# Two-stage transformer kernel on one core: the layers' steps in other orders, multi-query statistics one by one behind the maxima, the first queries' turned copy on VectorE

## The chip, the core and the metric

One core of one Trainium2 chip runs the kernel. The metric is the device time of one execution in microseconds (us). Engines are called by their names: TensorE (PE in the profile; PEld is its weight load), VectorE (DVE), ScalarE (ACT), GpSimd (POOL) and SyncE (SP), which issues transfers.

## What is computed

The input x is 8 sequences of 512 tokens with 128 features. Two blocks follow, each added to x behind a layer norm:

```python
x = x + _layernorm(_L0_attn_ref(_layernorm(x), ...))     # multi-query attention, 16 heads of 8, one k and v
x = x + _layernorm(_L0_ffn_ref(_layernorm(x), ...))      # six layers
# one of the six layers
x = attn_layer(shift_tokens(x), Wqkv[i], q_scale[i], k_scale[i], Wo[i]) + x
x = ffn_layer(shift_tokens(x), ln_g[i], ln_b[i], W1[i], b1[i], W2[i], b2[i]) + x
# attn_layer: 16 heads of 64; q and k are normalised to length 1, scaled, rotated;
# attention is causal within windows of 32 tokens and the window before
# ffn_layer: layer norm, x @ W1 in halves a and gate, a * gelu(gate) @ W2
```

All is float32. Where it can, the kernel splits an operand into a rounded part and a remainder (hi and lo) and multiplies in three passes.

## The kernel before

**Stages.** A constants stage, the multi-query stage (to about 650 us), the layers (about 670 to 3740 us) and an output stage. Each engine runs a program of its own, in the order in which it is written; engines meet by semaphores alone. `Events` counts them: `at(k, cycle)` is the value of a semaphore once k of its events of that cycle are done.

**Multi-query stage.** It goes through 8 batches of 512 tokens, in a loop whose body is `sequence`. Of each of 16 heads (`g` is a group of four, `i` a head in it) TensorE computes the scores in two layouts. `scores` writes four tiles (`qt`), alternately into the banks `score[0]` and `score[1]`; VectorE's `maxima` takes the row maxima, five heads (AHEAD) before `scoresT`, the other layout, uses them and ScalarE's `exps` takes exponentials. A score tile waits for the maximum of the tile two before it (`s_max`). Between heads VectorE does the three norms: 0 of the next batch's input, 1 of the batch before's projected output, 2 of its residual sum. Each is `mean_and_var` (four bn_stats, four bn_aggr, an addition), then a power on GpSimd (`inverse_deviation`, L272), then `normalised` (four tensor_scalar), one lump each behind the maxima of a head. At the end of a batch the next one's keys and queries are turned: `turn_keys` and `turn_queries` on TensorE into bank `turn[0]`; the keys are copied out half by ScalarE (`keys_turned`), half by VectorE (`other_keys`, L660), each of the four groups of queries by ScalarE (`queries_turned`, the first one behind the exponentials of head (3, 3)). TensorE's first score of the next batch waits for the first queries' copy.

**Layers.** A step (cycle) takes 256 tokens, that is two tiles of 128; 6 layers x 16 steps = 96 cycles. `CYCLE` writes out by hand, for each engine, the order of its tokens in a cycle. The number behind a token is the tile against the cycle's own, so that a negative one belongs to an earlier cycle's tile; tile 2 of one cycle is tile 0 of the next. On TensorE: Pq, Pk, Pv project (six matmuls each, L1228 to L1230) into the one PSUM tile `proj`; Tq, Tk turn rotated q and k (L1237); S scores (L1256), X turns the exponentials (L1263), V weights the values (L1277), O turns the result (L1284), W projects it (L1291); mean (L1301), var (L1307), spread (L1314), GG, AA (L1323 to L1325) and F4 (L1332) are the feed-forward layer. All but the projections, S and spread write a ring of two PSUM buffers in turn, so each waits until the one before the last is released (`RELEASE`). On ScalarE: XSa loads the projection's input, Qq and Qk square `proj` (L1384), EV copies the values out of it, EQ, EK, EX, EO copy ring buffers out, MK writes the mask, IG makes the guess for the inverse root (L1395), EXP the exponentials, GEL gelu with two table loads. On VectorE: Cq, Ck rotate (L1494, L1496), and wait for the square; Rq, Rk sum squares, MX takes maxima, SB subtracts them, RS sums and inverts, R weights, AM gates (L1591), WX and XN add to x (XN: L1597), XC, FV, XM belong to the norm. On GpSimd: Aq, Ak add (L1142), Mq, Mk scale (L1148), N is Newton's steps, XSd, XL remainders, FP a power. A projection waits until `proj` is rotated or copied. SyncE moves the values into `v_win` (VM). `NEXT_WEIGHTS` puts pieces of the next layer's weights (hi_, lo_ halves, turn_ tables) ahead of certain tokens, two and one cycles before a layer ends.

## Time and profile before

| | us |
|---|---|
| median of 3 timed runs | 3786.93 (3782.76 to 3786.98) |
| the profiled execution | 3777.28 |
| its span, first to last instruction | 3775.5 |

| engine | busy us | share of the span |
|---|---|---|
| PE | 3506.6 | 93% |
| PEld | 2890.2 | 77% |
| DVE | 2982.0 | 79% |
| ACT | 2678.1 | 71% |
| POOL | 2407.2 | 64% |

Busy time is that of the instructions' spans; matmuls are pipelined, so neighbours overlap and a busy TensorE is not TensorE at its peak. A shape's start-to-start step says what it costs. A value like "[0.17 <-DVE by_sin L1496]" behind a row is the idle time ahead of it and what ended that. The granted clock is given as a share of TensorE's full clock.

### The profile page before, as it was taken

Reading aid. Unit: us, or ns where it says so; the run is one execution under the profiler, and the core shown is the slowest. Engines: PE = TensorE matmul, PEld = TensorE weight load, DVE = VectorE, ACT = ScalarE, POOL = GpSimd, SP = SyncE. Lnnn points to the kernel's source line nnn. Section 1 sums busy time; section 2 is a strip of 40 time slices with the busy share of each in tenths; the row PEclk is TensorE's granted clock in tenths of the full one; section 3 lists DMA queues with packets and bytes.
Section 4 is the critical chain, followed back from the end, with each engine's and each line's share of the span. In section 5 each row is a group of like instructions: output and inputs, shape, how many; then the busy total and the mean of one; then the engine's idle time right before and its main releaser. Section 6 shows DMA issues by size and latency. Waiting matters only on the chain. (4 is left out here: it accounts for less than half of the span.)

```text
span 3775.5 us, 161676 instructions
## 1 busy us (share of the span) xinstructions
PE 3506.6 (93%) x67234; PEld 2890.2 (77%) x67234; DVE 2982.0 (79%) x4293; ACT 2678.1 (71%) x4155; POOL 2407.2 (64%) x2884
## 2 busy tenths in 40 slices
PE   5988898599999999999999999999999999999995
PEld 3555555378888888888888888888888888888884
DVE  4455554588888888888888888888888888888884
ACT  2444443377778788887878888888888888878872
POOL 1010000577777777787777777777877777777773
PEclk9999999799999999999999999999999999999997
DMA  1000000132222232222322223222232222222222
GB/s 55 4 3 3 5 3 6 40 91 68 67 68 66 73 93 69 70 65 74 90 67 67 67 72 90 67 67 67 72 90 67 67 69 65 74 67 70 69 66 63
DMA packets 161717, 227.93 MB, mean 60 GB/s; under 512 B 42258, under 2 KB 60632, under 8 KB 161496
## 3 DMA queue, kind: packets, MB, share of 16 engines
q1 hardware_dynamic: 161624, 226.85, 24.0%
q8 instruction: 38, 0.62, 0.1%
q14 instruction: 55, 0.45, 0.0%
HBM read 21.00 MB, written 4.19 MB: 7 GB/s over the span
## 5 line engine op out<-in xcount | busy, mean ns | idle before, releaser
L1142 POOL TENSOR_TENSOR by_cos<-by_cos,by_sin 128x1024 f32<-128x1024 f32 x384 | 916.4, 2386 | 38.5 <-DVE by_sin L1496 38.5
L1148 POOL TENSOR_TENSOR by_cos<-by_cos,norms 128x1024 f32<-128x1024 f32 x384 | 724.8, 1910 | 0.0
L1494 DVE TENSOR_TENSOR by_cos<-proj,turns 128x1024 f32<-128x1024 f32 x384 | 470.0, 1224 | 224.0 <-ACT squares L1384 223.4
L1228 PE MATMUL proj<-qkv_hi,xs_hib 128*128 128x512 f32 x1152 | 522.4, 453 | 52.5 <-DVE by_sin L1496 39.8
L1384 ACT ACTIVATE squares<-proj 128x1024 f32<-128x1024 f32 x384 | 392.4, 1022 | 174.1 <-PE proj L1230 168.3
L1364 ACT ACTIVATE vb<-proj 128x1024 f32<-128x1024 f32 x192 | 195.3, 1017 | 422.9 <-PE proj L1230 383.0
L1496 DVE TENSOR_TENSOR by_sin<-proj,turns 128x1024 f32<-128x1024 f32 x384 | 466.1, 1214 | 0.0
L1500 DVE TENSOR_REDUCE sumsb<-squares 128x16 f32<-128x1024 f32 x384 | 463.9, 1208 | 1.5 <-DVE w_lo L1563 1.5
L1229 PE MATMUL proj<-qkv_lo,xs_hib 128*128 128x512 f32 x1152 | 457.3, 397 | 1.3 <-issue 1.3
L1230 PE MATMUL proj<-qkv_hi,xs_lob 128*128 128x512 f32 x1152 | 458.0, 398 | 0.0
L1237 PE MATMUL ring<-ident,by_cos 128*128 128x128 f32 x3072 | 403.7, 275 | 1.7 <-POOL by_cos L1148 1.4
L1237 PEld LDWEIGHTS ring<-ident,by_cos 128*128 128x128 f32 x3072 | 351.2, 142 | 49.0 <-DVE attnb L1531 22.4
L668 DVE TENSOR_REDUCE a_row_max<-a_score 128x1 f32<-128x128 f32 (+3 forms) x512 | 238.1, 487 | 175.2 <-PE a_score L311 171.2
L1291 PE MATMUL ring<-attnT,wo 128*128 128x256 f32 x1536 | 347.6, 379 | 1.4 <-ACT attnT L1364 1.2
L1228 PEld LDWEIGHTS proj<-qkv_hi,xs_hib 128*128 128x128 f32 x1152 | 218.6, 190 | 141.0 <-DVE by_sin L1496 93.0
L1291 PEld LDWEIGHTS ring<-attnT,wo 128*128 128x128 f32 x1536 | 284.3, 190 | 36.6 <-issue 1.4
L1256 PE MATMUL score<-kTb,qTb 64*32 64x64 f32 x24576 | 286.2, 226 | 8.4 <-issue 8.4
L1277 PE MATMUL ring<-v_win,pTb 64*32 64x64 f32 x24576 | 285.6, 225 | 6.5 <-issue 6.5
L509 ACT ACTIVATE a_probs<-a_scoreT 128x512 f32<-128x512 f32 (+1 forms) x384 | 186.3, 532 | 142.5 <-PE a_scoreT L324 137.0
L1256 PEld LDWEIGHTS score<-kTb,qTb 64*32 64x32 f32 x24576 | 256.8, 105 | 27.4 <-issue 10.6
L272 POOL TENSOR_TENSOR a_rstdb<-a_varb,minus_half 128x4 f32<-128x4 f32 x24 | 24.2, 1008 | 397.4 <-DVE a_varb L622 397.4
L1277 PEld LDWEIGHTS ring<-v_win,pTb 64*32 64x32 f32 x24576 | 254.3, 105 | 25.5 <-issue 23.9
(174 smaller groups left out, 8217.5 us busy)
## 6 DMA issues: line engine op xcount, KB each, us to landing
v_win<-vb SPq DMA_DIRECT2D x1152, 128.0 KB, 2.4
v_win<-vb SPq DMA_DIRECT2D x768, 64.0 KB, 2.0
in_qkv<-L_ffn_Wqkv SPq DMA_DIRECT2D x12, 768.0 KB
wo<-L_ffn_Wo SPq DMA_DIRECT2D x6, 512.0 KB, 4.1
x_tok<-L_attn_x SPq DMA_DIRECT2D x8, 256.0 KB, 4.8
residual<-x_tok SPq DMA_DIRECT2D x8, 256.0 KB, 2.1
o_x<-residual SPq DMA_DIRECT2D x1, 2048.0 KB, 7.8
out<-o_x SPq DMA_DIRECT2D x8, 256.0 KB, 2.3
```

The lines of the kernel that those rows point to most:

```text
L1142: nc.gpsimd.tensor_tensor(both, both, by_sin[:, j, :], ALU.add).then_inc(e[f"{w_}_added"].sem, 1)
L1148: nc.gpsimd.tensor_tensor(heads, heads, inverse, ALU.mult).then_inc(e[f"{w_}_ready"].sem, 1)
L1228: nc.tensor.matmul(out, xs_hi[:, tile], qkv_hi[:, cols], start=True, stop=False)
L1229: nc.tensor.matmul(out, xs_hi[:, tile], qkv_lo[:, cols], start=False, stop=False)
L1230: last = nc.tensor.matmul(out, xs_lo[:, tile], qkv_hi[:, cols], start=False, stop=True)
L1237: last = nc.tensor.transpose(out[:, i * P:(i + 1) * P], by_cos[:, t % 2, j, i * P:(i + 1) * P], ident[:, :])
L1256: last = nc.tensor.matmul(score[queries, at:at + KEYS], qT[rows, t % 2, i, queries], keys, start=False, stop=True, skip_group_check=True)
L1277: last = nc.tensor.matmul(out[queries, at:at + DH], pT[rows, i, queries], v_win[rows, t % 2, n, i, :], start=True, stop=True)
L1291: last = nc.tensor.matmul(out[:, 0:HS], wo[:, i, :], attnT[:, i, :], start=(i == 0), stop=(i == PAIRS - 1))
L1494: nc.vector.tensor_tensor(of_heads(by_cos[:, t % 2, j, :]), heads, table(0), ALU.mult)
L1496: nc.vector.tensor_tensor(swapped, heads, table(1), ALU.mult).then_inc(e[f"{w_}_rotated"].sem, 1)
L1500: nc.vector.tensor_reduce(sums[:, t % 2, j, :, 0], squares[:, :].rearrange("p (h d) -> p h d", d=DH), AX.X, ALU.add).then_inc(e[f"{w_}_sum ...
```

## The change

It has three parts.

1. `CYCLE` gets other orders on the four computing engines, and `NEXT_WEIGHTS` other places. On TensorE, V:-2 goes to the front and Tq:0 from the front to behind Pq:2; mean goes behind X:-1; S:0 ahead of O:-2, V:-1 and var; W:-1 ahead of Tk:1. On ScalarE, EX:0 of the end becomes EX:-2 at the front; XSa:3 goes from the front to behind Qk:2; EQ:0, XF, FSQ and XH move. On VectorE, XC goes behind Rq:2, WX ahead of Rq:3, and MX:1 and SB:1 ahead of Rk:3 and XN. On GpSimd, Aq of the second tile goes to the front of the next cycle (Aq:1), Mq:0 behind XSd:2, Mk:1 behind XL. No work is added or removed.
2. In the multi-query stage a bn_stats stands behind each of the four maxima of a head, and the normalising instructions behind the second (tile 0), third (tile 1) and fourth (tiles 2 and 3) maximum of another head. What is left of the lump is `variance`. Since a norm's tiles stand in the maxima of the head at the same place, `normalised` now waits for the inverse deviation behind the second maximum instead of the fourth.
3. The copy of the first group of turned queries goes from ScalarE (`queries_turned(b, 0)`) to VectorE (`first_queries`), with an event of its own (`q_first`).

```diff
-        "t1_full": Events(sem("a_t1_full"), 5), "t1": Events(sem("a_t1"), 5), "k_half": Events(sem("a_k_half"), 1),
+        "t1_full": Events(sem("a_t1_full"), 5), "t1": Events(sem("a_t1"), 4), "q_first": Events(sem("a_q_first"), 1), "k_half": Events(sem("a_k_half"), 1),
...
-                turned(b, 0, stacked(g), "t1_full", ("t1", g + 2, 1))
+                turned(b, 0, stacked(g), "t1_full", ("t1", g + 1, 1) if g else ("q_first", 1, 1))
...
-                pe.wait_ge(e["t1"].sem, e["t1"].at(2, b + 1))
+                pe.wait_ge(e["q_first"].sem, e["q_first"].at(1, b + 1))
...
-                        elif (g, i) == (3, 3):
-                            queries_turned(b, 0)
...
+            def statistics(b, norm, tiles, after, t):
+
+                if t == 0:
+                    dve.wait_ge(padded, 2)
+                    if after:
+                        dve.wait_ge(e[after].sem, e[after].at(1, b))
+                last = nc.vector.bn_stats(stat6[:, norm, t, :], tiles[t])
+                if t == TILES - 1:
+                    last.then_inc(e[f"stats{norm}"].sem, 1)
...
+            def normal_tile(b, norm, out, tiles, t):
+
+                if t == 0:
+                    dve.wait_ge(e[f"rstd{norm}"].sem, e[f"rstd{norm}"].at(1, b))
+                return nc.vector.tensor_scalar(out[:, t, :], tiles[t], stat[:, norm, t, 0:1], rstd[:, norm, t:t + 1],
+                                               ALU.subtract, ALU.mult)
...
+            def first_queries(b):
+
+                dve.wait_ge(e["t1_full"].sem, e["t1_full"].at(2, b + 1))
+                nc.vector.tensor_copy(qT0[:, 0, :], turn[0][:, :]).then_inc(e["q_first"].sem, 1)
...
-            def maxima(b, g, i):
+            def maxima(b, g, i, behind=None):
...
+                    if behind:
+                        behind(qt)
...
+            def norm_behind(b, norm, out, tiles, done):
+
+                def behind(qt):
+                    for t in {1: (0,), 2: (1,), 3: (2, 3)}.get(qt, ()):
+                        last = normal_tile(b, norm, out, tiles, t)
+                        if t == TILES - 1:
+                            last.then_inc(e[done].sem, 1)
+                return behind
...
+                        behind = None
+                        if not first:
+                            if (g, i) == (0, 0):
+                                behind = lambda qt: statistics(b - 1, 1, projected, "proj", qt)
+                            elif (g, i) == (0, 1):
+                                behind = norm_behind(b - 1, 1, o, projected, "o")
+                            elif (g, i) == (0, 3):
+                                behind = lambda qt: statistics(b - 1, 2, tiles_of(b - 1), "x2", qt)
+                            elif (g, i) == (1, 0):
+                                behind = norm_behind(b - 1, 2, y, tiles_of(b - 1), "y")
+                        if not last:
+                            if (g, i) == (1, 3):
+                                behind = lambda qt: statistics(b + 1, 0, tiles_of(b + 1), None, qt)
+                            elif (g, i) == (2, 0):
+                                behind = norm_behind(b + 1, 0, xn, tiles_of(b + 1), "xn")
...
-    "PE": "Tq:0 V:-2 Pq:2 mean Tk:0 X:-1 O:-2 Pk:2 var V:-1 S:0 spread Pv:2 O:-1 Tq:1 Pq:3 Tk:1 W:-1 Pk:3 GG "
+    "PE": "V:-2 Pq:2 Tq:0 Tk:0 X:-1 mean Pk:2 S:0 O:-2 V:-1 var Pv:2 spread O:-1 Tq:1 Pq:3 W:-1 Tk:1 Pk:3 GG "
     "S:1 AA X:0 Pv:3 F4",
-    "Act": "XSa:2 XSa:3 EV:1 EQ:0 IG:1 XF EXP:-1 Qq:2 FSQ EK:0 EX:-1 MK:0 EO:-2 Qk:2 EV:2 EO:-1 EQ:1 Qq:3 IG:2 "
-    "MK:1 XH EXP:0 EK:1 Qk:3 GEL EX:0",
-    "DVE": "R:-2 XC Cq:2 Rq:2 RS:-1 FV Ck:2 R:-1 XM Rk:2 MX:0 SB:0 Cq:3 Rq:3 RS:0 WX:-1 Ck:3 AM Rk:3 XN MX:1 "
-    "SB:1",
-    "Pool": "Mq:0 XSd:2 N:1 Ak:1 Aq:2 FP Mq:1 Mk:1 XSd:3 Ak:2 XL N:2 Aq:3 Mk:2",
+    "Act": "EX:-2 XSa:2 EV:1 XF IG:1 EXP:-1 Qq:2 EQ:0 EK:0 MK:0 EX:-1 FSQ Qk:2 XSa:3 EO:-2 EV:2 EO:-1 XH EQ:1 "
+    "IG:2 Qq:3 EXP:0 MK:1 EK:1 Qk:3 GEL",
+    "DVE": "R:-2 Cq:2 Rq:2 XC RS:-1 Ck:2 FV R:-1 XM Rk:2 MX:0 SB:0 Cq:3 WX:-1 Rq:3 RS:0 Ck:3 AM MX:1 SB:1 Rk:3 "
+    "XN",
+    "Pool": "Aq:1 XSd:2 Mq:0 N:1 Ak:1 Aq:2 Mq:1 XSd:3 FP Ak:2 XL Mk:1 N:2 Mk:2",
...
-    "Act": {(-2, "Qq:3"): "hi_q1", (-2, "EK:1"): "hi_q0", (-2, "GEL"): "hi_k0", (-2, "EX:0"): "hi_k1",
-          (-1, "XSa:3"): "hi_v0", (-1, "EXP:-1"): "hi_v1"},
-    "DVE": {(-2, "WX:-1"): "lo_q0", (-2, "Rk:3"): "turn_3", (-2, "XN"): "lo_k1", (-2, "SB:1"): "lo_k0",
-          (-1, "Cq:2"): "turn_0 turn_1 turn_2"},
-    "Pool": {(-2, "XL"): "lo_q1", (-1, "N:1"): "lo_v0", (-1, "Aq:2"): "lo_v1"},
+    "Act": {(-2, "EXP:0"): "hi_q0", (-2, "EK:1"): "hi_q1", (-2, "GEL"): "hi_k0", (-1, "XSa:2"): "hi_v0",
+          (-1, "EV:1"): "hi_k1", (-1, "XF"): "hi_v1"},
+    "DVE": {(-2, "AM"): "lo_q0 turn_0 turn_1", (-2, "Rk:3"): "turn_2 turn_3", (-1, "R:-2"): "lo_k1",
+          (-1, "RS:-1"): "lo_v1"},
+    "Pool": {(-2, "Mk:2"): "lo_q1", (-1, "Aq:1"): "lo_k0", (-1, "XSd:2"): "lo_v0"},
```

## Rows read from the trace of the kernel before

**Rows 1.** Two stretches: length, busy us (xcount) of PE, PEld, DVE, ACT, POOL, clock, DMA, GB/s.
```profile
40.00:648.00 608.00, 541.43 (x3799) 347.76 (x3797) 333.00 (x999) 271.15 (x596) 57.31 (x29) 0.97 0.01 3
...
1000.00:3600.00 2600.00, 2542.12 (x55110) 2187.03 (x55109) 2272.08 (x2718) 2085.62 (x3078) 2011.80 (x2438) 1.00 0.29 72
```

**Rows 2.** Timeline of PE in one cycle of the layers: start us, us, what.
```profile
2020.51 1.04 PE L1237 MATMUL ring<-ident,by_cos 128*128 128x128 f32 x8
...
2021.48 1.48 PE L1277 MATMUL ring<-v_win,pTb 64*32 64x64 f32 x128
...
2022.89 0.50 PE L1228 MATMUL proj<-qkv_hi,xs_hib 128*128 128x512 f32 x1
...
2028.21 0.50 PE L1228 MATMUL proj<-qkv_hi,xs_hib 128*128 128x512 f32 x1
...
2030.14 1.48 PE L1277 MATMUL ring<-v_win,pTb 64*32 64x64 f32 x128
...
2031.53 1.47 PE L1256 MATMUL score<-kTb,qTb 64*32 64x64 f32 x128
...
2032.93 0.43 PE L1314 MATMUL ring<-ident,f_rstdb 128*128 128x128 f32 x2
...
2033.53 0.50 PE L1228 MATMUL proj<-qkv_hi,xs_hib 128*128 128x512 f32 x1 [0.17 <-DVE by_sin L1496]
...
2035.02 1.06 PE L1284 MATMUL ring<-ident,attnb 128*128 128x128 f32 x8
...
2035.92 1.04 PE L1237 MATMUL ring<-ident,by_cos 128*128 128x128 f32 x8
...
2036.71 0.48 PE L1228 MATMUL proj<-qkv_hi,xs_hib 128*128 128x512 f32 x1
...
2042.34 0.58 PE L1228 MATMUL proj<-qkv_hi,xs_hib 128*128 128x512 f32 x1
...
2048.61 0.48 PE L1228 MATMUL proj<-qkv_hi,xs_hib 128*128 128x512 f32 x1
...
2051.38 1.04 PE L1237 MATMUL ring<-ident,by_cos 128*128 128x128 f32 x8
```

**Rows 3.** Timeline of ACT and DVE behind the projection at 2022.89.
```profile
2024.76 1.01 ACT L1384 ACTIVATE squares<-proj 128x1024 f32<-128x1024 f32 x1
...
2025.80 1.22 DVE L1494 TENSOR_TENSOR by_cos<-proj,turns 128x1024 f32<-128x1024 f32 x1 [0.36 <-ACT squares L1384]
2026.94 1.22 DVE L1496 TENSOR_TENSOR by_sin<-proj,turns 128x1024 f32<-128x1024 f32 x1
```

**Rows 4.** Groups of instructions by line, whole span: busy us, mean ns, idle before.
```profile
L1591 DVE SCALAR_TENSOR_TENSOR hidden<-ring,ffn_col,hidden 128x256 f32<-128x256 f32 (+1 forms) x288 | 121.4, 477 | 30.8 <-PE ring L1325 30.2
...
L1395 ACT ACTIVATE norms<-floors,guess_bias 128x32 f32<-128x32 int32 x192 | 60.6, 316 | 0.0
...
L1597 DVE TENSOR_TENSOR xT<-ring,xT 128x256 f32 (+1 forms) x96 | 40.7, 424 | 94.2 <-PE ring L1332 94.2
...
L272 POOL TENSOR_TENSOR a_rstdb<-a_varb,minus_half 128x4 f32<-128x4 f32 x24 | 24.2, 1008 | 397.4 <-DVE a_varb L622 397.4
...
L660 DVE CAST a_kT<-a_turn 32x512 fp32r<-32x512 f32 x16 | 11.1, 693 | 7.1 <-PE a_turn L376 7.0
```

**Rows 5.** Timeline of PE at a boundary between two multi-query batches.
```profile
268.00 0.65 PE L376 MATMUL a_turn<-ident,a_qa 128*128 128x128 f32 x4 [0.18 <-DVE a_kT L660]
270.15 0.32 PE L310 MATMUL a_score<-a_kT,a_qT 128*128 128x128 f32 x1 [1.50 <-ACT a_qT L501]
```

**Rows 6.** Waits of PE, 286 to 325 us: us in total, times, longest.
```profile
PE a_score L310 <- DVE a_row_max L668: 3.5, 5, 0.9
```

**Rows 7.** Two stretches of the multi-query stage, columns as in rows 1.
```profile
290.00:303.00 13.00, 10.79 (x70) 7.50 (x68) 11.73 (x44) 7.01 (x15) 1.06 (x2) 1.00 0.05 20
...
344.00:348.00 4.00, 3.65 (x18) 1.81 (x22) 1.27 (x3) 0.22 (x1) 2.80 (x1) 0.52 0.00 0
```

**Rows 8.** A cycle in which the next layer's weights are prepared, columns as in rows 1.
```profile
1175.00:1207.00 32.00, 30.17 (x625) 25.38 (x627) 29.24 (x38) 25.82 (x41) 26.82 (x32) 1.00 0.27 66
```

More of the change, by code:

```diff
@@ L433, in sequence @@
                 pe.wait_ge(e["k1"].sem, e["k1"].at(1, b))
-                pe.wait_ge(e["t1"].sem, e["t1"].at(5, b))
+                pe.wait_ge(e["t1"].sem, e["t1"].at(4, b))
                 for g in range(GROUPS):
@@ L488, in _ @@
                 turn_queries(-1, g)
-            pe.wait_ge(e["t1"].sem, e["t1"].at(3, 0))
+            pe.wait_ge(e["t1"].sem, e["t1"].at(2, 0))
             for i in range(PER_GROUP):
@@ L596, in _ @@
             keys_turned(-1)
-            for g in range(GROUPS):
+            for g in range(1, GROUPS):
                 queries_turned(-1, g)
@@ L605, in _, with variance @@
             dve.wait_ge(padded, 2)
-            def mean_and_var(b, norm, tiles, after=None):
-                stats = e[f"stats{norm}"]
-                dve.wait_ge(padded, 2)
-                if after:
-                    dve.wait_ge(e[after].sem, e[after].at(1, b))
-                for t, tile in enumerate(tiles):
-                    last = nc.vector.bn_stats(stat6[:, norm, t, :], tile)
-                last.then_inc(stats.sem, 1)
+            def statistics(b, norm, tiles, after, t):
[6 more added lines that the diff above has]
+                    last.then_inc(e[f"stats{norm}"].sem, 1)
+            def variance(b, norm):
+                stats = e[f"stats{norm}"]
                 dve.wait_ge(stats.sem, stats.at(1, b))
@@ L623, in mean_and_var @@
                                         ALU.add).then_inc(e[f"var{norm}"].sem, 1)
+            def mean_and_var(b, norm, tiles, after=None):
+                for t in range(TILES):
+                    statistics(b, norm, tiles, after, t)
+                variance(b, norm)
+            def normal_tile(b, norm, out, tiles, t):
[3 more added lines that the diff above has]
+                                               ALU.subtract, ALU.mult)
             def normalised(b, norm, out, tiles):
-                dve.wait_ge(e[f"rstd{norm}"].sem, e[f"rstd{norm}"].at(1, b))
-                for t, tile in enumerate(tiles):
-                    last = nc.vector.tensor_scalar(out[:, t, :], tile, stat[:, norm, t, 0:1], rstd[:, norm, t:t + 1],
-                                                   ALU.subtract, ALU.mult)
+                for t in range(TILES):
+                    last = normal_tile(b, norm, out, tiles, t)
                 return last
@@ L692, in add_output @@
                 nc.vector.tensor_tensor(four, four, o[:, :, :], ALU.add).then_inc(e["x2"].sem, 1)
+            def norm_behind(b, norm, out, tiles, done):
+                def behind(qt):
+                    for t in {1: (0,), 2: (1,), 3: (2, 3)}.get(qt, ()):
+                        last = normal_tile(b, norm, out, tiles, t)
+                        if t == TILES - 1:
+                            last.then_inc(e[done].sem, 1)
+                return behind
             def sequence(b, first=False, last=False):
@@ L697, in sequence @@
                         then = g * PER_GROUP + i + AHEAD
+                        behind = None
[13 more added lines that the diff above has]
+                                behind = norm_behind(b + 1, 0, xn, tiles_of(b + 1), "xn")
                         if then < MQA_H:
-                            maxima(b, then // PER_GROUP, then % PER_GROUP)
+                            maxima(b, then // PER_GROUP, then % PER_GROUP, behind)
                         if i == 2 and g + 1 < GROUPS:
@@ L706, in sequence @@
                             if (g, i) == (0, 0):
-                                mean_and_var(b - 1, 1, projected, "proj")
-                            elif (g, i) == (0, 1):
-                                normalised(b - 1, 1, o, projected).then_inc(e["o"].sem, 1)
+                                variance(b - 1, 1)
                             elif (g, i) == (0, 2):
@@ L712, in sequence @@
                             elif (g, i) == (0, 3):
-                                mean_and_var(b - 1, 2, tiles_of(b - 1), "x2")
-                            elif (g, i) == (1, 0):
-                                normalised(b - 1, 2, y, tiles_of(b - 1)).then_inc(e["y"].sem, 1)
+                                variance(b - 1, 2)
                         if last:
@@ L718, in sequence @@
                         if (g, i) == (1, 3):
-                            mean_and_var(b + 1, 0, tiles_of(b + 1))
-                        elif (g, i) == (2, 0):
-                            normalised(b + 1, 0, xn, tiles_of(b + 1)).then_inc(e["xn"].sem, 1)
+                            variance(b + 1, 0)
                         elif g == 3 and i < 2:
@@ L725, in sequence @@
                             other_keys(b)
+                        elif (g, i) == (3, 3):
+                            first_queries(b)
                 if last:
@@ L748, in _ @@
             other_keys(-1)
+            first_queries(-1)
             for i in range(PER_GROUP):
```

## The prediction

> **What bounds the kernel now.** I read the page's slices first: TensorE is the fullest engine everywhere but in the fill around 650 to 780 us. Then two stretches by windows [rows 1]: in the layers TensorE is busy 2542 of 2600 us at a granted clock of 1.00, VectorE 87%, ScalarE 80%, GpSimd 77%; in the multi-query stage (40 to 648 us) TensorE is busy 541 of 608 us at a mean clock of 0.97. So time can only come from TensorE's gaps, and from work that a low clock stretches. The chain of waits on the page covers only the output stage and doesn't help; the timeline of one cycle does [rows 2]. The 96 cycles of the layers repeat with one period: transposes of Tq:0 start at 2020.51 and again at 2051.38, 30.87 us. An uninterrupted projection with what follows it starts its successor at a fixed step, so I take start-to-start steps rather than durations (matmuls overlap by some 0.1 us).
>
> **The loop through `proj`.** One PSUM tile `proj` serves all six projections of a cycle. Behind Pq (2022.89) ScalarE squares it (2024.76, 1.01 us), VectorE rotates it twice (2025.80 and 2026.94, 1.22 us each, end 2028.16) and only then Pk may start: 2028.21 [rows 2, 3]. That is 5.32 us from a projection that is rotated to the next, whatever TensorE does meanwhile. Between Pq:2 and Pk:2 the old order has mean, Tk, X and O to fill it; their issue steps are too short, so it waits some 0.7 us. Between Pk:2 (2028.21) and Pv:2 (2033.53) it has var, V, S and spread; again 5.32, with a wait on the rotation in the row of 2033.53. Elsewhere the work between two projections is longer than the rotation.
>
> **Layers: the new order, stretch by stretch** (steps from rows 2; numbers behind tokens are tiles).
> - Pq:2 to Pk:2. Old and new hold about 3.0 us of work (new: Tq:0, Tk:0, X:-1, mean), less than the 3.8 that the rotation leaves. Stays 5.32.
> - Pk:2 to Pv:2. New: S:0, O:-2, V:-1, var. Pk with var 2028.21 to 2030.14 = 1.93; S 2031.53 to 2032.93 = 1.40; O 2035.02 to 2035.92 = 0.90; V 2021.48 to 2022.89 = 1.41. Sum 5.64, over 5.32: TensorE is no longer late for the rotation, and 0.32 longer than before.
> - Pv:2 to Pq:3. Old O:-1 and Tq:1, 2033.53 to 2036.71 = 3.18. New has spread too, two of the transposes of which Tq takes 0.11 each (0.89/8): 3.40. ScalarE's copy of `proj` is done long before.
> - Pq:3 to Pk:3 (W and Tk:1 change places) and Pk:3 to Pv:3 (unchanged): 2036.71 to 2048.61 = 11.90, the latter with GEL's wait.
> - Pv:3 to the next Pq:2. Old F4, Tq:0, V:-2: 2048.61 to 2051.38 and 2020.51 to 2022.89 = 5.15. Tq:0 (2020.51 to 2021.48 = 0.97) has moved behind Pq:2, into the wait: 4.18.
>
> Sum 5.32 + 5.64 + 3.40 + 11.90 + 4.18 = 30.44, against 30.87: 0.43 us a cycle. The gain is not O or V as such: what stood in an over-full stretch (Tq:0 between Pv:3 and Pq:2) goes where TensorE waited. I then followed each queue through the new cycle with Pq:2 at 0. Ring buffers: X:-1 needs EQ:0, which starts behind Qq:2 and ends at 3.7, so X starts then and not at 3.25, but ends before Pk:2 at 5.32. Mean needs EK:0 (4.7). EO:-2 frees var's buffer at 10.3, var starts at 10.4. XM frees Tq:1's buffer at 13.2, Tq:1 starts at 13.4. EX:-2 now opens ScalarE's cycle and has V:-2 waiting a microsecond after it. GpSimd's new order keeps Mq:0 0.8 us and Mk:1 1 us ahead of their transposes. SyncE's transfers into v_win are issued, as now, most of a cycle before their V. Everything hides, but with 0.1 to 0.3 us in five places; I take the sum and keep 0.1 to 0.7 us a cycle for the range. With some 91 full cycles: 39 us (9 to 64).
>
> **Layer boundary.** The same 16 weight pieces (ScalarE 6, GpSimd 3, VectorE 3 and 4 tables) go to other places. A preparing cycle now has TensorE busy 30.17 of 32 us [rows 8], so such a cycle loses about 1.1 us to the regular one, and I count about three in each of five boundaries. VectorE gets lo_q0 and two tables ahead of AM, where F4 waits for them, but loses the run of three ahead of the first Cq:2. I take nothing, plus or minus 8 us in all.
>
> **Multi-query stage, first queries.** At each of seven batch boundaries TensorE has the first queries turned by 268.65 and waits until 270.15: the copy is queued on ScalarE behind three exponentials [rows 5]. VectorE is idle there. Its nearest copy out of PSUM (32 partitions, 512 columns) is 0.69 us [rows 4], so the copy is there at 268.65 + 0.1 + 0.69 = 269.5 and 0.65 us goes: 7 x 0.65 = 4.6. Behind it on VectorE stand only the maxima, which need that copy anyway.
>
> **Statistics one by one.** In the 39 us around a batch's norms TensorE waits 3.5 us in five waits for maxima behind a lump of VectorE work [rows 6]. Four of them lie where VectorE is itself nearly full (11.73 of 13 us [rows 7]): spreading out the same instructions frees at most the 1.3 us of its gaps. And the new order makes a wait: the first normalised tile stands behind the second maximum, while the inverse deviation takes GpSimd 1.0 us [rows 4] from the variance on; VectorE would stand about 0.5 us, with two maxima and so TensorE's next score behind it, at norms 1 and 2. I take no gain there (-0.6 to +1.0), and 0.7 us at norm 0, where TensorE's heads are longer than VectorE's load: 7 x 0.7 = 5. The Trainium skill, Perfetto Trace Analysis, Optimizing Scalar/DVE Operations, says that breaking up instructions may let work complete sooner if Vector isn't saturated but causes bubbles. By it nearly all 3.5 us would go, 25 us in seven batches; the row of the 13 us speaks against its condition. That is a rival below.
>
> **Clock.** The trace grants 0.52 (a mix of the levels 2.4 and 1.2 GHz) in 344 to 348 us [rows 7], just behind a boundary wait of the kind of rows 5; such a drop stands behind six of the seven. Its 3.65 us of work would take some 1.9 less at 2.4 GHz. With 0.85 instead of 1.5 us idle some drops should go: I take half, 6 x 1.9 / 2 = 5 (0 to 11).
>
> **Sum.** Layers 39, first queries 5, statistics 5, clock 5: 54 us. The profiled execution took 3777.3 (span 3775.5), 9.6 less than the median 3786.9 of the three timed runs. 3777.3 - 54 = 3723; against the median 3733.
>
> **Rivals.**
> - The fill is paid elsewhere: a second loop becomes the bound. Rk:3 and its floors now stand behind SB:1, and the guess IG:1, EXP:-1 and Qq:2 wait for them. From Pk:3: rotation done 5.27; AM 3 x 0.477 = 1.43 [rows 4]; MX, SB, Rk at 1.22 each; floors and guess 0.32 each; EXP and square at 1.01 each; Cq 2.36: 15.4 and some 0.3 of handoffs to Pk:2. From there TensorE needs 5.64 + 3.40 and Pq:3 to Pk:3, 5.63: 30.4, as much as TensorE's own sum. At 0.4 more the layers gain nothing and only the 15 us of the first stage are left: 3772.
> - The same loop on the other side, slower: if it closes at over 31.04 us (30.87 and 15/91), the kernel is slower than before. It has about 20 handoffs between three engines; 0.05 more at each and the misfit of one VectorE operation make 31.3: 0.43 x 91 = +39, less 15: 3811. For it speaks that slack is nearly nothing; against it, that the old order had VectorE wait for F4 1 us in each cycle (94 us in 96 [rows 4]) with MX:1 and SB:1 behind it, and that XN now stands last.
> - The skill's rule holds, all maxima waits go: 20 us more, 3713.
> - The change doesn't do what it says: TensorE's wait at the boundary isn't for the copy but for what comes next on ScalarE (exponentials, then V). Costs the 10 us of queries and clock, 3743; inside the forecast.
>
> **How the numbers follow.** Forecast 3733 with 0.66 (its terms alone: 3705 to 3765); layers gain nothing 0.12; slower 0.11; rule 0.11. Range 3702 to 3775, leaving out 0.11 above, some of the 3772 case, and little below. 0.2% is 7.6 us, about what a measurement can tell from no change. Faster: 0.66, 0.11 and half of 0.12, say 0.82; same 0.07; slower 0.11.
>
> **What would show it.** Period between two Tq:0 at 30.3 to 30.6; no wait on by_sin ahead of Pv:2; Pq:2 to Pk:2 still 5.3. If EXP:-1 ends later than Pq:2, the second loop binds. At the batch boundary the wait ends 0.6 earlier, by VectorE; mean clock of 40 to 648 over 0.97; VectorE standing for a_rstdb before a_ob and a_yb. The forecast is wrong if the period stays at 30.9, or if boundary cycles grow past 33.

## The result and the profile after

| us | median | lowest to highest | runs |
|---|---|---|---|
| before | 3782.06 | 3777.72 to 3786.98 | 6 |
| after | 3756.27 | 3744.30 to 3766.11 | 6 |

The ratio is 0.9927, with a 95% interval of 0.9916 to 0.9939: faster by 26 us, less than half of the 54 that were forecast, and inside the range. The profiled execution of after has a span of 3742.5 us where that of before had 3775.5, 33 less; it is the fastest of its six. In after the lines of the layers stand 42 further down (L1228 is L1270, L1237 is L1279), the maxima are L687 and the maximum's neighbours L611 (bn_stats), L637 (normalising), L671 (the first queries' copy) and L678 (the keys' copy).

The two stretches of [rows 1] in after:

```profile
40.00:648.00 608.00, 542.52 (x3819) 349.40 (x3818) 344.96 (x1038) 271.57 (x594) 66.68 (x40) 0.96 0.01 5
...
1000.00:3600.00 2600.00, 2533.26 (x55104) 2177.23 (x55103) 2302.20 (x2717) 2111.84 (x3080) 2003.81 (x2442) 1.00 0.29 72
```

In the second row TensorE is idle 67 of 2600 us (2600 - 2533.26), where it was 58: there are new waits in the layers. In the first row a fixed window misleads: the stage is shorter now and 40 to 648 us holds the start of the fill (the pipeline of the layers starting up) with its low clock; to 626 us the clock is 0.98.

**Where the 33 us are.** I cut both traces at the first and the last matmul of mean (L1301 before, L1343 after): 779.02 and 3729.63 in before, 750.64 and 3696.86 in after. So 28.4 us went ahead of the layers and only 4.4 of their 2950.6 us. The forecast had it the other way round: 15 and 39. One pair of profiles is thin for the second number: with the old orders three profiles (before, e2_queries, e3_stats) have 2950.6 to 2960.7 us there, with the new ones four (after, e0_again, e1_layers, e7_later) 2946.2 to 2950.2, so the layers gave 4 us by this pair and some 10 by the middle of either group. The steps from one mean matmul to the next split the 4.4 again. The regular cycle (its median) fell from 30.93 to 30.68 (medians of 95 steps), worth 95 x 0.25 = 24 us; but at each of the five layer boundaries the eight cycles around it now take 7.4 us more than regular ones, where it was 3.3 (at the last one 9.7 and 5.3): 5 x 4.1 = 20 us back.

**The cycle.** TensorE's timeline of the cycle of [rows 2] in after (start us, us, what):

```profile
2020.30 1.48 PE L1319 MATMUL ring<-v_win,pTb 64*32 64x64 f32 x128
2021.71 0.50 PE L1270 MATMUL proj<-qkv_hi,xs_hib 128*128 128x512 f32 x1
...
2023.21 1.91 PE L1279 MATMUL ring<-ident,by_cos 128*128 128x128 f32 x16
2025.54 1.09 PE L1305 MATMUL ring<-ident,probs 128*128 128x128 f32 x8 [0.42 <-ACT qTb L1406]
2026.46 0.69 PE L1343 MATMUL ring<-xfb,mean_of 128*128 128x256 f32 x2
2026.94 0.50 PE L1270 MATMUL proj<-qkv_hi,xs_hib 128*128 128x512 f32 x1
...
2028.53 1.48 PE L1298 MATMUL score<-kTb,qTb 64*32 64x64 f32 x128
2029.95 1.09 PE L1326 MATMUL ring<-ident,attnb 128*128 128x128 f32 x8
2030.97 1.48 PE L1319 MATMUL ring<-v_win,pTb 64*32 64x64 f32 x128
2032.39 0.61 PE L1349 MATMUL ring<-mean_of,fsqb 128*128 128x1 f32 x4
2032.85 0.48 PE L1270 MATMUL proj<-qkv_hi,xs_hib 128*128 128x512 f32 x1
...
2036.22 0.48 PE L1270 MATMUL proj<-qkv_hi,xs_hib 128*128 128x512 f32 x1
...
2048.11 0.48 PE L1270 MATMUL proj<-qkv_hi,xs_hib 128*128 128x512 f32 x1
```

The wait on the rotation ahead of Pv:2 (2032.85) is gone, and X's 0.42 on EQ stands where the forecast put it. EXP:-1 ends at 2023.28 on ScalarE and Qq:2 starts at 2023.47, when the projection is done. Start to start: Pq:2 to Pk:2 5.23 (forecast 5.32), Pk:2 to Pv:2 5.91 (5.64), Pv:2 to Pq:3 3.37 (3.40), Pq:3 to Pv:3 11.89 (11.90), and to the next Pq:2 4.28 (4.18). One stretch carries the miss. In it P takes 1.59 to the next start, S 1.42, O 1.02, V 1.42, var 0.46. In the old order the forecast had read P with var as 1.93 (now 2.05) and O as 0.90.

**The layer boundary.** TensorE's waits in 1122 to 1157 us, across a cycle that prepares the next layer's weights:

```profile
PE ring L1374 <- DVE hidden L1633: 1.3, 1, 1.3
PE ring L1279 <- DVE xT L1639: 1.0, 1, 1.0
PE ring L1279 <- DVE attnb L1573: 0.6, 1, 0.6
PE ring L1305 <- ACT hidden L1506: 0.5, 1, 0.5
```

Three of the four, 2.9 us, are for VectorE, and the longest is that of F4 for AM, which now has lo_q0 and two tables ahead of it. What VectorE and GpSimd do there:

```profile
1142.15 2.37 POOL L1184 TENSOR_TENSOR by_cos<-by_cos,by_sin 128x1024 f32<-128x1024 f32 x1
...
1142.56 2.51 DVE L1585 TENSOR_TENSOR qkv_lo<-in_qkv,qkv_hi 128x512 fp32r<-128x512 f32 x1
...
1144.99 0.75 DVE L1593 SCALAR_TENSOR_TENSOR turns<-tables_sb,in_qs 128x256 f32<-128x256 f32 x2
...
1145.66 0.47 DVE L1633 SCALAR_TENSOR_TENSOR hidden<-ring,ffn_col,hidden 128x256 f32<-128x256 f32 x1
```

And the same instruction over the whole span, first in after, then in before (duration in ns: shortest, median, longest):

```profile
L1585 DVE TENSOR_TENSOR qkv_lo<-in_qkv,qkv_hi x18: 679/2492/2509, 646.3 to 3151.3; 128x512 fp32r<-128x512 f32 x18
```

```profile
L1543 DVE TENSOR_TENSOR qkv_lo<-in_qkv,qkv_hi x18: 628/720/1748, 673.7 to 3173.5; 128x512 fp32r<-128x512 f32 x18
```

An instruction of 0.7 us takes 2.5 where it meets GpSimd's addition of 2.4 us, and ends 0.55 us behind it (1145.07 against 1144.52). Two of the three in a boundary do: lo_q0, and lo_v1 16 us later, behind which TensorE waits 1.45 us for the rotation ahead of Pv. The Trainium skill, SBUF — State Buffer, section SBUF: two separate sides, says that VectorE and GpSimd share a pair of ports under an exclusive lock: a VectorE instruction with two SBUF inputs and a GpSimd instruction that reads SBUF don't run together, and whichever comes second waits for the whole of the other. The trace agrees: 0.68 becomes 2.51 only where such a GpSimd instruction is running. This rule spoke against the new places, and the prediction had not weighed it.

**The multi-query stage.** A batch boundary of after (260.76 answers [rows 5]), and the first norm behind it:

```profile
259.25 0.65 PE L376 MATMUL a_turn<-ident,a_qa 128*128 128x128 f32 x4 [0.18 <-DVE a_kT L678]
...
259.94 0.69 DVE L671 CAST a_qT<-a_turn 128x512 fp32r<-128x512 f32 x1 [0.82 <-PE a_turn L376]
...
260.76 0.32 PE L310 MATMUL a_score<-a_kT,a_qT 128*128 128x128 f32 x1 [0.86 <-DVE a_qT L671]
```

```profile
285.94 0.62 DVE L687 TENSOR_REDUCE a_row_max<-a_score 128x1 f32<-128x128 f32 x2
287.14 0.41 DVE L637 TENSOR_SCALAR a_ob<-a_turn,a_stat,a_rstdb 128x128 f32<-128x128 f32 x1 [0.57 <-POOL a_rstdb L272]
```

The boundary wait ends by VectorE and lasts 0.86 instead of 1.50. VectorE stands 0.57 for the inverse deviation, as forecast. TensorE's waits for maxima over 40 to 640 us, in before, then in after:

```profile
PE a_score L310 <- DVE a_row_max L668: 34.2, 66, 0.9
```

```profile
PE a_score L310 <- DVE a_row_max L687: 18.5, 58, 0.6
```

15.7 us of such waiting are gone, where the forecast had 5. The 39 us of [rows 6], at the same place in a batch of after (423 to 462 us), show where:

```profile
PE a_score L310 <- DVE a_row_max L687: 1.3, 4, 0.5
```

That is 2.2 us less in each batch: 0.6 at norm 0, as forecast (0.79 to 0.22), and 1.5 at norms 1 and 2 (2.68 to 1.22), where the forecast had taken no gain. GpSimd's addition to the turned keys marks each batch once. Of the six batches between the second mark and the eighth, only one of before went by without a low clock, 268.10 to 342.29, 74.2 us; in after three did, 71.6 us each:

```profile
333.75 4.54 POOL L281 TENSOR_TENSOR a_kT<-a_kT,ones 128x2048 fp32r<-128x2048 f32 x1 [23.22 <-DVE a_kT L678]
...
405.38 4.54 POOL L281 TENSOR_TENSOR a_kT<-a_kT,ones 128x2048 fp32r<-128x2048 f32 x1 [23.23 <-DVE a_kT L678]
...
477.07 4.53 POOL L281 TENSOR_TENSOR a_kT<-a_kT,ones 128x2048 fp32r<-128x2048 f32 x1 [23.23 <-DVE a_kT L678]
```

(The batch from 333.75 to 405.38 and the next; the third ends at 548.71.) That is 2.6 us a batch without any help of the clock. The six batches together take 458.6 us in before and 436.7 in after, 21.9 less: 6 x 2.6 = 15.6 by the shorter waits, and 6.3 because fewer and shorter stretches of low clock fall into them.

### The profile page after: what moved, and what is told of

Read it like the earlier page. It is cut to its first block and busy times, and to the rows that moved or that the text cites. A ratio compares the mean times of both kernels' runs of the same rounds, so it can differ in the third digit from the quotient of the medians.

```text
span 3742.5 us, 161624 instructions
## 1 busy us (share of the span) xinstructions
PE 3489.5 (93%) x67234; PEld 2872.1 (77%) x67234; DVE 3020.8 (81%) x4301; ACT 2705.2 (72%) x4147; POOL 2398.5 (64%) x2884
## 5 line engine op out<-in xcount | busy, mean ns | idle before, releaser
L1190 POOL TENSOR_TENSOR by_cos<-by_cos,norms 128x1024 f32<-128x1024 f32 x384 | 733.5, 1910 | 13.0
L1270 PE MATMUL proj<-qkv_hi,xs_hib 128*128 128x512 f32 x1152 | 512.4, 445 | 49.2 <-DVE by_sin L1538 40.2
L1279 PE MATMUL ring<-ident,by_cos 128*128 128x128 f32 x3072 | 385.3, 273 | 8.4 <-DVE xT L1639 5.5
L1279 PEld LDWEIGHTS ring<-ident,by_cos 128*128 128x128 f32 x3072 | 351.0, 142 | 34.3 <-issue 7.6
L687 DVE TENSOR_REDUCE a_row_max<-a_score 128x1 f32<-128x128 f32 (+3 forms) x512 | 240.3, 486 | 127.9 <-PE a_score L311 121.6
L1333 PEld LDWEIGHTS ring<-attnT,wo 128*128 128x128 f32 x1536 | 292.3, 190 | 44.0 <-ACT attnT L1406 1.4
L1198 POOL TENSOR_TENSOR xs_lob<-xsb,xs_hib 128x128 fp32r<-128x128 f32 x192 | 88.3, 460 | 347.7 <-ACT xs_hib L1406 347.7
L1270 PEld LDWEIGHTS proj<-qkv_hi,xs_hib 128*128 128x128 f32 x1152 | 219.1, 190 | 109.9 <-DVE by_sin L1538 63.3
```

The source lines that it names most:

```text
L1190: nc.gpsimd.tensor_tensor(heads, heads, inverse, ALU.mult).then_inc(e[f"{w_}_ready"].sem, 1)
L1270: nc.tensor.matmul(out, xs_hi[:, tile], qkv_hi[:, cols], start=True, stop=False)
L1279: last = nc.tensor.transpose(out[:, i * P:(i + 1) * P], by_cos[:, t % 2, j, i * P:(i + 1) * P], ident[:, :])
L1333: last = nc.tensor.matmul(out[:, 0:HS], wo[:, i, :], attnT[:, i, :], start=(i == 0), stop=(i == PAIRS - 1))
```

## The experiments

The theory drawn from these profiles had four parts: the new order of the layers gives 0.25 us a cycle and not 0.43, since steps ahead of the small matmuls are longer; the weight pieces cost 4 us a boundary, of which the shared port is a part; the statistics give more than their term; and the clock makes the rest. The rivals are named with each run. Each run was timed against the kernel before on the same chip.

| kernel | median us | ratio to before, 95% interval | regular cycle | boundary, over regular |
|---|---|---|---|---|
| after, again (e0_again) | 3750.71 | 0.9909 [0.9896, 0.9923] | 30.68 | 7.4 |
| e1_layers | 3775.56 | 0.9985 [0.9975, 0.9994] | 30.68 | 7.4 |
| e2_queries | 3779.14 | 0.9993 [0.998, 1.0005] | 30.93 | 3.3 |
| e3_stats | 3773.82 | 0.9979 [0.997, 0.9987] | 30.95 | 3.2 |
| e4_ports | 3748.40 | 0.9911 [0.9891, 0.9931] | 30.68 | 5.8 |
| e5_together | 3743.43 | 0.9900 [0.9885, 0.9914] | 30.50 | 9.2 and 7.6 |
| e6_weights | 3738.39 | 0.9879 [0.9865, 0.9894] | 30.68 | 4.2 |
| e7_later | 3758.50 | 0.9924 [0.9906, 0.9942] | 30.68 | 7.4 |
| e9_both | 3731.09 | 0.9868 [0.9851, 0.9885] | 30.50 | 4.3 |
| e10_gelu | 3740.16 | 0.9895 [0.9875, 0.9916] | 30.50 | 8.1 to 9.2 |

The last two columns come from the steps between mean matmuls in each profile. The last is for the first four boundaries; the fifth varies more (7.5 to 12.8 us with the new orders). They agree to 0.1 us between profiles of the same order, save where a low clock falls into a preparing cycle: one boundary of e7_later (9.0 us), two of the first four of e5_together and all of e10_gelu. The first stage moves more: the layers of the kernels that share after's first stage begin anywhere from 746 to 762 us, by the number of batches with a low clock. So an edit in the layers is read from its cycles first and from the median second.

**e1_layers: part 1 alone** (the new `CYCLE` and `NEXT_WEIGHTS` in the kernel before).

```diff
-    "PE": "Tq:0 V:-2 Pq:2 mean Tk:0 X:-1 O:-2 Pk:2 var V:-1 S:0 spread Pv:2 O:-1 Tq:1 Pq:3 Tk:1 W:-1 Pk:3 GG "
+    "PE": "V:-2 Pq:2 Tq:0 Tk:0 X:-1 mean Pk:2 S:0 O:-2 V:-1 var Pv:2 spread O:-1 Tq:1 Pq:3 W:-1 Tk:1 Pk:3 GG "
...
+    "DVE": {(-2, "AM"): "lo_q0 turn_0 turn_1", (-2, "Rk:3"): "turn_2 turn_3", (-1, "R:-2"): "lo_k1",
+          (-1, "RS:-1"): "lo_v1"},
```

> The kernel before with the layers' new orders and weight places alone. From the two traces: the regular cycle goes from 30.90 to 30.68 us (75 regular cycles, 17 us less) and the three irregular cycles at each of five layer boundaries from 3.4 to 7.4 us in excess (20 us more); the fill gains some 5. Theory (the layers bring next to nothing, the gain is the first stage's): 0 to 9 us less than before. Rival (the orders bring the gain and the first stage's smaller time is chance of the clock): over 20 us less.

Measured: 7 us less than before (3782.49 in 29 runs), cycle 30.68, 7.4 us over at each boundary; from the first to the last mean matmul 2947.2 against 2950.6. The largest term of the sum, 39 us, is worth 3 us by the profile and 7 by the medians, and it is the layers by themselves that lose it, not something that the other two parts do to them.

**e2_queries: part 3 alone.**

```diff
-                        elif (g, i) == (3, 3):
-                            queries_turned(b, 0)
...
+                        elif (g, i) == (3, 3):
+                            first_queries(b)
```

> The kernel before with the first queries' copy on VectorE alone. The boundary wait goes from 1.50 to 0.86 us seven times, 4.5 us. Theory: on top of that the clock drops behind that wait go from six to two or fewer, some 2 us each: 8 to 14 us less than before. Rival (the drops have nothing to do with that wait): 4 to 5 us less, and still five or six drops behind the boundaries.

Measured: 3.3 us less, with an interval that includes no change. The seven waits fell from 10.5 us in sum to 6.0:

```profile
PE a_score L310 <- DVE a_qT L656: 6.0, 7, 0.9
```

A batch without a low clock takes 73.5 us (from GpSimd's addition at 490.30 to that at 563.84) against 74.2: 0.7 a batch, the size in the sum. None of its low stretches stands right behind a boundary wait any more, but four stand later in the batch, so the clock gave nothing on top. The size is the rival's, 4 to 5 us, and not the theory's 8 to 14.

**e3_stats: part 2 alone.**

```diff
-                                mean_and_var(b - 1, 1, projected, "proj")
-                            elif (g, i) == (0, 1):
-                                normalised(b - 1, 1, o, projected).then_inc(e["o"].sem, 1)
...
+                            if (g, i) == (0, 0):
+                                behind = lambda qt: statistics(b - 1, 1, projected, "proj", qt)
+                            elif (g, i) == (0, 1):
+                                behind = norm_behind(b - 1, 1, o, projected, "o")
```

> The kernel before with the statistics and the normalising instructions behind single maxima alone. TensorE's waits for maxima at score L310 fell from 34.2 to 18.5 us between the two traces of the first stage. Theory: this part alone brings those 16 us, less what VectorE stands for the inverse deviation (0.57 us a time, in 14 places): 8 to 16 us less. The prediction's term (no gain at norms 1 and 2, 0.7 at norm 0): 5 us less. Drops of the clock behind the boundary wait stay at five to seven.

Measured: 8.7 us less. The waits for maxima fall to 19.4 us, VectorE stands for the inverse deviation 4.0 us at each of the three norms:

```profile
PE a_score L310 <- DVE a_row_max L684: 19.4, 60, 0.6
```

```profile
DVE a_ob L639 <- POOL a_rstdb L272: 4.0, 7, 0.6
```

In its profile six batches take 75.0 or 75.1 us, each with two low stretches. Columns as in [rows 7]; the first stretch is behind the boundary wait of 1.50, the second 17 us later:

```profile
345.00:349.00 4.00, 3.86 (x22) 1.21 (x21) 1.23 (x3) 0.00 (x0) 2.28 (x1) 0.60 0.00 0
...
361.00:365.00 4.00, 4.00 (x21) 3.12 (x19) 0.72 (x2) 0.33 (x1) 0.00 (x0) 0.73 0.00 0
```

The profiled execution was 9 us longer than this kernel's median, so its clock is not typical; the waits are. A batch of before with two low stretches of the same length at nearly the same places (419.18 to 496.19 us) takes 77.0 us. Like against like, then, part 2 alone gives 1.9 us a batch. The three parts alone give 6.9 + 3.3 + 8.7 = 19 us; together they gave 26 and, once more on another chip, 33 (e0_again). The intervals of the four ratios together leave some 8 us open either way, so the surplus of 7 is no finding and that of 14 is one. It goes the way of the clock, since the profiles of after and e0_again have three and five of the six batches free of a low clock where before has one; that nothing else makes it isn't shown.

**e4_ports: after, with the two residuals moved away from GpSimd's additions.**

```diff
-    "DVE": {(-2, "AM"): "lo_q0 turn_0 turn_1", (-2, "Rk:3"): "turn_2 turn_3", (-1, "R:-2"): "lo_k1",
-          (-1, "RS:-1"): "lo_v1"},
+    "DVE": {(-2, "WX:-1"): "lo_q0", (-2, "AM"): "turn_0 turn_1", (-2, "Rk:3"): "turn_2 turn_3", (-1, "R:-2"): "lo_k1",
+          (-1, "Cq:2"): "lo_v1"},
```

> The changed kernel with two of VectorE's three subtractions of the next weights (lo_q0, lo_v1) moved from where GpSimd is in an addition of two SBUF tensors (2.4 us long) to where GpSimd does Newton's short steps: lo_q0 ahead of WX:-1, lo_v1 ahead of Cq:2. Same number of instructions. Theory (a VectorE instruction with two SBUF inputs stands until GpSimd's two-input instruction is over, 2.5 us in place of 0.68): these two fall from 2.5 to about 0.7 us each, and the boundary's excess from 7.4 to 3.5 to 5 us, in all 12 to 20 us less than the changed kernel, 3736 to 3744. Rival (the pieces are slow by themselves, or it is only the place in the chain ahead of AM): durations stay at 2.5 us, or the excess stays over 6 us.

```profile
L1585 DVE TENSOR_TENSOR qkv_lo<-in_qkv,qkv_hi x18: 679/682/693, 653.8 to 3149.9; 128x512 fp32r<-128x512 f32 x18
```

Measured: all 18 residuals take 0.68 us, and a boundary costs 5.8 us instead of 7.4. The direction is right and the cause of the 2.5 us is shown (same instruction, same data, other neighbour). But the run doesn't take the port out of the boundary. In the place that lo_q0 left, the two tables now meet the same addition of GpSimd, and they too have two inputs in SBUF:

```profile
1151.62 2.94 DVE L1593 SCALAR_TENSOR_TENSOR turns<-tables_sb,in_qs 128x256 f32<-128x256 f32 x2
...
1151.72 2.56 POOL L1184 TENSOR_TENSOR by_cos<-by_cos,by_sin 128x1024 f32<-128x1024 f32 x1
```

The pair took 0.75 us in after and takes 2.94 here; the second of them takes 2.60 alone, at every boundary. So AM starts no more than 0.2 us earlier behind the rotation, and the first preparing cycle stays 4.0 us over the regular one. The whole gain of 1.6 us comes from the second preparing cycle, where TensorE no longer waits 1.45 us for the rotation: lo_v1 had stood ahead of it and was longer by 1.8. Its place was changed with its neighbour, so even these 1.6 us aren't split between the two. Of the 4.1 us by which a boundary had grown, 1.6 went here and 2.5 stay, the rest of the port's cost among them.

**e0_again: after, unchanged, beside the next three.**

> The changed kernel once more, beside the others on the same chip. Theory (what varies from run to run is where the clock drops in the first stage, not the layers): cycle 30.68 and boundary excess 7.4 us as in the first trace, but another list of drops before 650 us, and a median of 3750 to 3760.

Measured: the cycle and the first four boundaries are those of after to 0.1 us; five batches of 71.6 or 71.7 us. It has low stretches at other places than after's own profile. One of them is in the last boundary, which takes 12.7 us where it took 9.7: a cycle there has a granted clock of 0.9, behind a wait of 2.1 us, so the layers take 2950.2 us from mean to mean against after's 2946.2. So the clock moves the layers too, by a few us.

**e5_together: after, with S:0 and V:-1 next to each other.**

```diff
-    "PE": "V:-2 Pq:2 Tq:0 Tk:0 X:-1 mean Pk:2 S:0 O:-2 V:-1 var Pv:2 spread O:-1 Tq:1 Pq:3 W:-1 Tk:1 Pk:3 GG "
+    "PE": "V:-2 Pq:2 Tq:0 Tk:0 X:-1 mean Pk:2 O:-2 S:0 V:-1 var Pv:2 spread O:-1 Tq:1 Pq:3 W:-1 Tk:1 Pk:3 GG "
```

> The changed kernel with S:0 moved behind O:-2, so that S:0 and V:-1, the two blocks of small 64x32 matmuls, stand side by side again as in the kernel before. Theory (a block of small matmuls costs some 0.1 us more at each of its edges with full ones, and the changed order has four such blocks in a cycle where the one before had three): P 1.50, O 1.02, S 1.40, V 1.42, var 0.46 = 5.80 in place of 5.91, cycle 30.55 to 30.6, 7 to 12 us less than the changed kernel. Rival (the 0.24 us by which the cycle is longer than forecast are handoffs between engines, whatever stands side by side): 30.66 to 30.70.

The stretch Pk:2 to Pv:2:

```profile
2026.75 0.50 PE L1270 MATMUL proj<-qkv_hi,xs_hib 128*128 128x512 f32 x1
...
2028.24 1.03 PE L1326 MATMUL ring<-ident,attnb 128*128 128x128 f32 x8
2029.21 1.48 PE L1298 MATMUL score<-kTb,qTb 64*32 64x64 f32 x128
2030.60 1.48 PE L1319 MATMUL ring<-v_win,pTb 64*32 64x64 f32 x128
2032.01 0.60 PE L1349 MATMUL ring<-mean_of,fsqb 128*128 128x1 f32 x4
2032.47 0.48 PE L1270 MATMUL proj<-qkv_hi,xs_hib 128*128 128x512 f32 x1
```

5.72 us instead of 5.91, with the same instructions and no wait in either. P takes 1.49 to the next start where O follows and 1.59 where S follows. The cycle fell by 0.18. So the steps do depend on the neighbour: the change had made four blocks of the small matmuls out of three, and putting two together brings it back to three. Two of the first four boundaries grew by 1.8 us, to 9.2, and the other two by 0.2. The trace says why: in the former the clock fell behind the wait of 1.6 us for the rotation in the second preparing cycle (0.66 from 1165 to 1170 us, 0.95 over the cycle), in the latter the same wait left it at 1.00. The boundary of 9.0 us in e7_later has the same mark (0.95). So it is the clock, and not the new order.

**e6_weights: after, with most of VectorE's pieces in other places.**

```diff
-    "DVE": {(-2, "AM"): "lo_q0 turn_0 turn_1", (-2, "Rk:3"): "turn_2 turn_3", (-1, "R:-2"): "lo_k1",
-          (-1, "RS:-1"): "lo_v1"},
+    "DVE": {(-2, "WX:-1"): "lo_q0 turn_0 turn_1", (-1, "R:-2"): "lo_k1", (-1, "Cq:2"): "turn_2 turn_3 lo_v1"},
```

> The changed kernel with all of VectorE's pieces of the next weights out of the chain from Ck:3 to Qq:2: lo_q0, turn_0 and turn_1 ahead of WX:-1, turn_2, turn_3 and lo_v1 ahead of the first Cq:2, where VectorE waits 1.15 us for the squares anyway. Theory (the boundary's excess is the length of what stands in that chain, and the port made two pieces 1.8 us longer): excess from 7.4 to 2.5 to 4 us, 17 to 24 us less than the changed kernel, 3732 to 3740. Rival (the excess comes from ScalarE's hi pieces ahead of EV:1 and GEL): over 5 us as with lo_q0 and lo_v1 alone (5.8).

In the same stretch as above the waits for VectorE are gone, and that for ScalarE's gelu is 1.2 us where it was 0.5:

```profile
PE ring L1304 <- ACT hidden L1505: 1.2, 1, 1.2
PE ring L1304 <- ACT qTb L1405: 0.4, 1, 0.4
```

Measured: a boundary costs 4.2 us, nearly the old 3.3; the layers take 2931.0 us from mean to mean, 15 less than in after (5 x 3.2 = 16). So most of the 20 us given back at the boundaries hang on where six of VectorE's seven pieces stand. The new places also keep them clear of GpSimd's long additions (from the first boundary on no residual takes over 0.74 us), so this run takes away the length of the pieces and the port's share at once. An estimate from the rows of 1142 to 1146 us: without the port lo_q0 would end 1.8 us earlier, and F4 waited 1.3. The port may thus be the larger part; a run with the pieces in their places and GpSimd's addition moved would tell, and there is none.

**e7_later: after, with each normalising step one maximum later.**

```diff
-                    for t in {1: (0,), 2: (1,), 3: (2, 3)}.get(qt, ()):
+                    for t in {2: (0,), 3: (1, 2, 3)}.get(qt, ()):
```

> The changed kernel with the first normalised tile behind the third maximum and the other three behind the fourth, in place of the second, third and fourth. Theory (VectorE stands 0.57 us for the inverse deviation behind the second maximum, and the scores wait for that): the standing goes, TensorE's waits for maxima fall from 18.5 us to 12 to 16, and a batch without a drop of the clock falls from 71.6 to 71.0 to 71.4 us: 2 to 5 us less, hardly to be told in the time. Rival (the lump of three behind the fourth maximum costs what the standing did): 71.6 to 71.9.

Measured: VectorE no longer stands for the inverse deviation, and the waits for maxima are 17.2 us instead of 18.5. Whether the time follows stays open: all seven batches of the profile had low stretches (74.4 to 75.7 us), and its runs spread over 25 us.

**e9_both: e5 and e6 together.**

```diff
+    "PE": "V:-2 Pq:2 Tq:0 Tk:0 X:-1 mean Pk:2 O:-2 S:0 V:-1 var Pv:2 spread O:-1 Tq:1 Pq:3 W:-1 Tk:1 Pk:3 GG "
...
+    "DVE": {(-2, "WX:-1"): "lo_q0 turn_0 turn_1", (-1, "R:-2"): "lo_k1", (-1, "Cq:2"): "turn_2 turn_3 lo_v1"},
```

> The changed kernel with both: S:0 beside V:-1, and VectorE's pieces of the next weights out of the chain. Theory (edges of small-matmul blocks and pieces in the chain are separate costs): cycle 30.50 us as with the first alone, boundary excess 4.2 to 6 (4.2 with the second alone; the first alone had 7.6 to 9.3 where it had 7.4 before, since a shorter cycle hides less), 20 to 30 us less than the changed kernel: 3724 to 3734. Rival (both ate the same slack): 3736 to 3742, no better than either.

Measured: 3731.09 us against 3782.57, 51 less. Cycle 30.50 and 4.3 us a boundary, the values of e5 and e6; the layers take 2918.4 us, 28 less than after's 2946.2. With both terms mended the change gives about what was forecast. It is the fastest kernel of this study.

**e10_gelu: e9 with ScalarE's piece taken away from gelu.**

```diff
-    "Act": {(-2, "EXP:0"): "hi_q0", (-2, "EK:1"): "hi_q1", (-2, "GEL"): "hi_k0", (-1, "XSa:2"): "hi_v0",
+    "Act": {(-2, "EXP:0"): "hi_q0", (-2, "EK:1"): "hi_q1", (-1, "XSa:2"): "hi_k0 hi_v0",
```

> As e9_both, with ScalarE's hi_k0 taken from ahead of GEL to behind EX:-2 of the next cycle. With the pieces of VectorE gone, TensorE's longest wait of the preparing cycle is 1.2 us at X:0 for GEL, of which the piece ahead of GEL (0.55 us step on ScalarE) should be a half. Theory: that wait goes to 0.6 us and the excess falls by 0.5 a boundary, 2 to 3 us in all, which the cycles show and the time hardly. Rival: the delay moves to EV:1 and Pq:2, excess unchanged or larger.

TensorE's waits in 1620 to 1700 us, in e9, then in this kernel:

```profile
PE ring L1304 <- ACT qTb L1405: 1.6, 3, 0.8
PE ring L1304 <- ACT hidden L1505: 1.2, 1, 1.2
```

```profile
PE proj L1269 <- POOL xs_lob L1197: 3.8, 1, 3.8
PE ring L1304 <- ACT qTb L1405: 0.8, 2, 0.4
PE ring L1304 <- ACT hidden L1505: 0.7, 1, 0.7
```

GpSimd there:

```profile
1637.92 1.28 POOL L1217 TENSOR_TENSOR qkv_lo<-in_qkv,qkv_hi 128x512 fp32r<-128x512 f32 x1 [4.82 <-ACT qkv_hi L1405]
```

Gelu's wait fell from 1.2 to 0.7, and a new one of 3.8 us took its place: hi_k0 now comes so late that GpSimd stands 4.82 us ahead of its residual lo_k0, with xs_lob, which a projection needs, queued behind it. Two of VectorE's residuals are long again (1.77 and 2.38 us). A boundary costs 8 to 9 us, twice that of e9. A part of that is the clock: behind the wait of 3.8 us it falls at all five boundaries (0.57 from 1644 to 1648 us), for longer at those of 9.1 and 9.2 us than at those of 8.1; in e9 it stays at 1.00 there.

## Why the prediction was right in the whole and wrong in its parts

- **The cover of the rotation** (layers, the loop through `proj`): right. No wait ahead of Pv:2, Pq:2 to Pk:2 at 5.23, four of the five stretches within 0.1 us.
- **Pk:2 to Pv:2 at 5.64**: too small by 0.27, all of the 0.24 by which the cycle came out over 30.44 and a little more; 5.91 measured. The step that failed is taking P with var (1.93) and O (0.90) from the old order, where other matmuls followed them. The new order puts S and V behind them, and e5 shows that the neighbour alone is worth 0.18 us a cycle. With 0.25 instead of 0.43 the 39 us become 24, and the period of 30.68 lies just over the 30.3 to 30.6 that were named as its sign.
- **Layer boundary, "nothing, plus or minus 8 us"**: wrong, +20 us. I saw that VectorE would get three pieces ahead of AM with F4 waiting, and set against it the run of three that it lost, without costing either, and without asking what GpSimd does beside them. e6 wins back 15 of the 20 us by moving VectorE's pieces alone. How much of that is the pieces' length and how much the port isn't shown: e4 moved the port's cost from lo_q0 to a table and won 1.6 of the 4.1 us at each boundary. The mark that I had named for a wrong forecast, boundary cycles over 33 us, was passed: the longest takes 34.7.
- **First queries, 4.6 us**: right. 0.64 a boundary by the wait, 0.7 a batch by e2.
- **Statistics, 5 us**: too small. 15.7 us of waits for maxima went. A batch without a low clock lost 2.6 us in all, 0.7 of them by e2, so 1.9 a batch, 13 us; e3's batches against one of before with as much low clock give the same 1.9. The argument failed that where VectorE is nearly full (11.73 of 13 us, [rows 7]) nothing is to be won but its gaps: the waits at norms 1 and 2 fell from 2.68 to 1.22 us a batch, since a maximum no longer stands behind a lump. e3 shows that part 2 alone does it (19.4 us of such waits, after 18.5); which half of it, the statistics or the normalising, wasn't taken apart. The stand for the inverse deviation came as forecast, 0.57 us, and cost little. The rival by which all waits for maxima go (20 us more than forecast) got 8 of its 20. It stood beside a rule of the Trainium skill, Perfetto Trace Analysis, Optimizing Scalar/DVE Operations, that breaking up instructions may let work complete sooner. Here no instruction was broken up but lumps of several were; with that difference the trace agrees in direction, and even where VectorE had little idle time.
- **Clock, 5 us**: the direction fits, the count was wrong, and the size isn't shown by itself. (The term's own working, 6 x 1.9 / 2, gives 5.7; nothing hangs on that.) I had written that a low clock stood behind six of the seven boundary waits; in before's profile three stand right behind one, the others come later in their batch. Over the profiles with the wait of 1.50 us 13 of 21 boundaries have one right behind, over those with 0.86 us 8 of 63. The 21 are fewer cases than they look, since e1_layers has its low stretches at before's places to 0.1 us. And the later ones don't vanish (e2 has four), so the gain differs from run to run. The kernel's first stage gave 19 to 22 us by the medians (26 less the 7 of e1, or less the 4 of the layers in the first pair of profiles); queries and statistics make 4.6 and 13 of it, and 1 to 4 are left for the clock.
- **The second loop** (floors, IG:1, EXP:-1, Qq:2; 3772): did not bind. EXP:-1 ends 0.2 us ahead of Qq:2's start. The median of 3756 lies between the forecast and that rival's time, for other reasons. **The slower loop** (3811) did not come.

So the sum of 54 had the layers too large by 35 (15 in the steps, 20 at the boundaries) and the statistics too small by 8. That the range held is owed to its width: had the statistics given only their 5, the time would have been some 3764, still inside, with the main term far off.

## What to carry to other kernels

A step from start to start holds for its neighbours of the time: when an order is turned round, look for the same pair in the trace, and where it isn't there add the difference that other pairs show. Work that is moved in a rare cycle is no rounding error when the regular cycle is won by tenths: 4 us at five places took back as much as 95 cycles gave. Before a VectorE instruction with two inputs in SBUF is moved, look at what GpSimd does at the new place, and at which instruction comes to stand beside it at the old one.
